# Expert rows weighed inside the expert loop, and the two rows of a token added on GpSimd ahead of the last normalization

## The reference

```
x: 6250 nodes x 256, 100000 edges with 96 features, sorted by dst
n  = layernorm(x)
x1 = x + n + relu([n, sum, max, mean of the node's edges, u] @ W1 + b1) @ W2 + b2
h  = layernorm(x1)
logits = h @ gate_w + gate_b               # 16 experts
(v1, v2), (e1, e2) = top_k(logits, 2);  w = softmax([v1, v2])
moe = w[0] * expert(e1, h) + w[1] * expert(e2, h)      # expert(e, h) = relu(h @ w1[e] + b1[e]) @ w2[e] + b2[e]
y = h + moe
out = x1 + layernorm(y) * gamma + beta
```

## Time and profile before

| | value |
|---|---|
| median of 3 executions | 1328.63 us |
| the profiled execution | 1334.45 us, span 1332.7 us |
| PE busy | 1185.9 us (89%) |
| DVE / ACT / POOL busy | 788.0 / 646.1 / 773.3 us |
| expert loop, about | 772 to 1221 us |
| final stage, about | 1223 to 1333 us |

### The profile page before, as it was taken

How to read it: one execution, slowest core, us unless ns; L and a number is a source line. 1 busy time by engine, 2 the same in 40 slices (tenths; PEclk the granted TensorE clock), 3 DMA queues, 4 the chain that set the end, 5 groups by cost and what they waited for, 6 DMA issues and landing times.

```text
span 1332.7 us, 28448 instructions
## 1 busy us (share of the span) xinstructions
PE 1185.9 (89%) x6684; PEld 1003.7 (75%) x6685; DVE 788.0 (59%) x3039; ACT 646.1 (48%) x1969; POOL 773.3 (58%) x1061
## 2 busy tenths in 40 slices
PE   2003999999999999999999989999999999999798
PEld 1003888888888888878888888899999999997343
DVE  4999999899799899903534014542222222222886
ACT  5963556655665665655664332223333333333554
POOL 4876666666666667666754235556666666663222
PEclk7555999999999999989999989999999999998555
DMA  9986677768758775592110348856666666664763
GB/s 313 287 269 232 201 275 284 283 237 318 256 215 294 276 239 189 218 334 80 47 45 28 115 155 296 269 174 205 212 212 204 211 212 211 210 212 123 244 203 93
DMA packets 131029, 282.67 MB, mean 212 GB/s; under 512 B 25609, under 2 KB 38283, under 8 KB 130821
## 3 DMA queue, kind: packets, MB, share of 16 engines
q1 hardware_dynamic: 93937, 218.40, 48.3%
q0 software_dynamic: 26048, 43.47, 10.4%
q10 hardware_dynamic: 10964, 19.96, 4.4%
HBM read 167.27 MB, written 114.25 MB: 211 GB/s over the span
## 4 chain that ended last, share of the span: by engine, by line
PE 63%; DMA 10%; issue 9%; POOL 8%; ACT 7%; POOLq 2%; DVE 1%; ACTq 1%; SPq 0%; DVEq 0%
PE ps L1158 14%; PE ps L1166 13%; PE ps L1048 8%; PE ps L1034 7%; PE ps L1036 7%; DMA mem<-piece_carry,mem 4%; PE ps L1199 3%; PE ps L1201 3%; POOL mem L571 2%; POOL mem L572 2%; PE ps L1144 2%; DMA mem<-x_normed,mem 2%; DMA mem<-in_dst_dram,mem 2%; POOL mem L554 2%; ACT mem L728 1%
## 5 line engine op out<-in xcount | busy, mean ns | idle before, releaser
L924 ACT ACTIVATE mem<-ps,mem 128x128 f32<-128x128 f32 x452 | 128.9, 368 | 306.8 <-PE ps L1158 304.8
L1158 PEld LDWEIGHTS ps<-mem 128*128 128x128 f32 x1808 | 221.4, 194 | 7.9 <-issue 3.0
L1158 PE MATMUL ps<-mem 128*128 128x128 f32 x1808 | 223.9, 278 | 1.5 <-issue 1.5
L1034 PE MATMUL ps<-mem 128*128 128x250 f32 x800 | 208.5, 383 | 13.5 <-ACT mem L826 11.9
L1166 PE MATMUL ps<-mem 128*128 x904 | 215.7, 382 | 2.8 <-issue 2.6
L1253 DVE TENSOR_TENSOR_SCAN mem<-ps,mem 128x80 f32<-128x80 f32 x960 | 207.9, 297 | 0.3
L1257 DVE TENSOR_TENSOR_SCAN mem<-ps,mem 128x80 f32<-128x80 f32 x960 | 207.8, 302 | 0.0
L1036 PE MATMUL ps<-mem 128*128 128x250 f32 x800 | 204.4, 378 | 0.0
L664 POOL DMA_INDIRECT expert_rows<-mem x113 | 113.5, 1004 | 126.9 <-DVE mem L1515 112.6
L1048 PE MATMUL ps<-mem 128*125 128x256 f32 x800 | 181.0, 379 | 0.7 <-ACT mem L826 0.7
L1166 PEld LDWEIGHTS ps<-mem 128*128 128x128 f32 x904 | 163.5, 191 | 22.7 <-issue 4.9
(11 more groups left out here) (252 smaller groups left out, 1696.1 us busy)
## 6 DMA issues: line engine op xcount, KB each, us to landing
mem<-in_L_ffn_w_dram SPq DMA_DIRECT2D x129, 512.0 KB, 9.4
run_sum<-mem SPq DMA_DIRECT2D x80, 480.0 KB
run_max<-mem SPq DMA_DIRECT2D x80, 480.0 KB
mem<-in_edge_attr_dram SPq DMA_DIRECT2D x72, 480.0 KB, 8.0
mem<-expert_rows SPq DMA_DIRECT2D x22, 512.0 KB, 5.4
x_rows<-mem ACTq DMA_DIRECT2D x25, 256.0 KB, 4.0
x_normed<-mem ACTq DMA_DIRECT2D x25, 256.0 KB
mem<-in_x_dram ACTq DMA_DIRECT2D x24, 256.0 KB, 4.1
```

The source lines that it names most:

```text
L924: ins = act.activation(hT[b][:, c, :], bank(2 + b, c * P, (c + 1) * P), ACT.Relu, bias=eb1c[:, bass.ds(e, 1), c])
L1034: pe.matmul(h, W1x[:, c, hc * P:(hc + 1) * P], XT[b][:, c, :], start=(c == 0), stop=False)
L1158: ins = pe.matmul(bank(2 + b, f * P, (f + 1) * P), w1now[q][:, c, f * P:(f + 1) * P], XgT[b][:, c, :], start=(c == 0), stop=(c == DC - 1))
```

## The change

The weight of a row is now a property of its slot. The one-hot products carry two values, the code of the row and its weight: `hot_rows` writes a second scaled one-hot beside the first, `early_slots` multiplies 172 columns instead of 86, `late_slots` 118 instead of 59, and `slot_tables` stores the weights as `wslot`. For that the exponential and `choice_weights` are done in two parts: for the early tiles in ACT's step 20 and before DVE's first `hot_rows`, for the late ones after ACT's tile 13 and DVE's tile 16. In the loop ACT multiplies the result of `expert2` in PSUM by `wslot` (`weigh_y`), and `take_y`, which now waits for ACT, adds the bias times `wslot`. In the final stage GpSimd adds the two rows of a token (`sum_rows`; those of batch n+2 stand ahead of the gamma product of batch n), and DVE adds the sum with one instruction per batch. DVE's `finish(n-1)` now comes after `moments(n+1)`; before, `finish(n)` did. ACT does `normed_again(n+2)` behind `last_norm(n)`, where it did `normed_again(n+1)` ahead of `deviation(n)`.

```diff
-    SLOTS_AT = 352
+    SLOTS_AT = 320
+            def sum_rows(n):
+                a = 2 * (BATCHES[n][1] - BATCHES[n][0])
+                pool.wait_ge(fy_got[n % DEEP], (n // DEEP + 1) * 32)
+                pool.tensor_tensor(FY[n % DEEP][0][0:NT, 0:a], FY[n % DEEP][0][0:NT, 0:a], FY[n % DEEP][1][0:NT, 0:a], ALU.add).then_inc(f_sum, 1)
...
+            sum_rows(0)
+            sum_rows(1)
             for n in range(len(BATCHES)):
+                if n + 2 < len(BATCHES):
+                    sum_rows(n + 2)
                 times_gamma(n)
...
+            def odds(part):
+                c = (slice(LC, TILES), slice(0, LC))[part]
+                act.wait_ge(gap_ready, part + 1)
+                act.activation(v0[:, 1, c], v0[:, 0, c], ACT.Exp).then_inc(e_gap, 1)
...
+            def weigh_y(i, b):
+                act.wait_ge(y_psum, i + 3)
+                act.activation(bank(6 + b, 0, D), bank(6 + b, 0, D), ACT.Identity, scale=wslot[:, bass.ds(i, 1)]).then_inc(y_weighed, 1)
+
+            def expert_step(i, g, b):
+                expert_relu(i, g, b)
+                weigh_y(i - 1, 1 - b)
...
             normed_again(0)
+            normed_again(1)
             for n in range(len(BATCHES)):
-                if n + 1 < len(BATCHES):
-                    normed_again(n + 1)
                 deviation(n)
                 last_norm(n)
+                if n + 2 < len(BATCHES):
+                    normed_again(n + 2)
...
-                        ins = pe.matmul(bank(7, SLOTS_AT, SLOTS_AT + KINDS), OL[n % HOT][:, m, :], OH[n % HOT][:, m, :],
+                        ins = pe.matmul(bank(7, SLOTS_AT, SLOTS_AT + 2 * KINDS), OL[n % HOT][:, m, :], OH[n % HOT][:, m, :],
...
-                pe.matmul(bank(5, P, P + OPEN), VT, Sel, start=True, stop=False)
+                pe.matmul(bank(5, P, P + 2 * OPEN), zeros[0:NT, 0:P], ones[0:NT, 0:2 * OPEN], start=True, stop=False)
+                for n in range(2):
+                    pe.matmul(bank(5, P + n * OPEN, P + (n + 1) * OPEN), VT[:, n], Sel, start=False, stop=False)
...
-                    st.mark(dve.scalar_tensor_tensor(out=high[n % HOT][:, m, :], in0=numbers[0:NT, 0:kinds], scalar=hi[:, kk, j:j + 1],
-                                                     in1=code[:, kk, c0 + j:c0 + j + 1].to_broadcast([NT, kinds]), op0=ALU.is_equal, op1=ALU.mult))
+                    for half, value in enumerate((code, wsel)):
+                        st.mark(dve.scalar_tensor_tensor(out=high[n % HOT][:, m, half * kinds:(half + 1) * kinds], in0=numbers[0:NT, 0:kinds], scalar=hi[:, kk, j:j + 1],
+                                                         in1=value[:, kk, c0 + j:c0 + j + 1].to_broadcast([NT, kinds]), op0=ALU.is_equal, op1=ALU.mult))
...
+                op(dve.tensor_copy(wslot[:, c], weight))
...
             places((Oa, Ob), rank, Rk, loq, hiq)
+            choice_weights(early, 0)
...
-                dve.wait_ge(y_psum, i + 3)
+                dve.wait_ge(y_weighed, i + 1)
                 if not isinstance(i, int) or i >= 2:
                     dve.wait_ge(yo_stored[b], g * 16)
-                dve.tensor_tensor(YO[b], bank(6 + b, 0, D), eb2bc[:, bass.ds(e, 1), :].rearrange("p o d -> p (o d)"), ALU.add).then_inc(y_ready, 1)
+                dve.scalar_tensor_tensor(out=YO[b], in0=eb2bc[:, bass.ds(e, 1), :].rearrange("p o d -> p (o d)"), scalar=wslot[:, bass.ds(i, 1)],
+                                         in1=bank(6 + b, 0, D), op0=ALU.mult, op1=ALU.add).then_inc(y_ready, 1)
...
                     late_experts(1)
+                    choice_weights(late, 1)
...
-            def add_expert(n, kk):
+            def add_experts(n):
...
+                dve.wait_ge(f_x2, n + 1)
+                dve.wait_ge(f_sum, n + 1)
+                f1.mark(dve.tensor_tensor(FS[b][:, 0:a], FS[b][:, 0:a], FY[n % DEEP][0][0:NT, 0:a], ALU.add))
                 f1.wait()
...
-            add_expert(0, 0)
-            add_expert(0, 1)
+            last = len(BATCHES) - 1
+            add_experts(0)
             moments(0)
             for n in range(len(BATCHES)):
-                if n + 1 < len(BATCHES):
-                    add_expert(n + 1, 0)
+                if n < last:
+                    add_experts(n + 1)
                 scale_shift(n)
-                if n + 1 < len(BATCHES):
-                    add_expert(n + 1, 1)
+                if n < last:
                     moments(n + 1)
-                finish(n)
+                if n:
+                    finish(n - 1)
+            finish(last)
```

More of the change, by code:

```diff
@@ L220, in gnn_moe_kernel @@
         wsel = k.take(2, TILES, parts=NT)
+        wslot = k.take(SLOT_TILES)
         IX = k.take(TILES, 2, parts=NT, dt=U32)
@@ L293, in gnn_moe_kernel @@
         OL = [a.take(OB, P, parts=NT) for _ in range(HOT)]
-        OH = [a.take(OB, KINDS, parts=NT) for _ in range(HOT)]
+        OH = [a.take(OB, 2 * KINDS, parts=NT) for _ in range(HOT)]
         a = Area(mem, WORK_END, TOTAL)
@@ L386, in gnn_moe_kernel @@
         fy_got = [sem(f"final_y_got{i}") for i in range(DEEP)]
-        f_x2, f_step, f_read, f_var, f_sd, f_stat, f_norm, f_scaled, f_z, f_out = (sem(f"final_{n}") for n in ("x2", "step", "y_read", "var", "sd", "stat", "norm", "scaled", "residual", "out"))
+        f_x2, f_sum, f_step, f_read, f_var, f_sd, f_stat, f_norm, f_scaled, f_z, f_out = (sem(f"final_{n}") for n in ("x2", "sum", "step", "y_read", "var", "sd", "stat", "norm", "scaled", "residual", "out"))
         pads_zeroed = sem("pads_zeroed")
@@ L917, in _ @@
                 gnn_step(i, i // 2, i % 2)
-            in_pairs(act, MACROS, lambda i, g, b: gnn_step(i, g, b, EARLY_M + MACROS - i), ahead=3, first=EARLY_M + 2)
+            for i in range(EARLY_M + 2, MACROS):
+                gnn_step(i, i // 2, i % 2)
+                if i == EARLY_M + 2:
+                    odds(0)
             def expert_relu(i, g, b):
@@ L934, in _ @@
             expert_relu(1, 0, 1)
+            weigh_y(0, 0)
             write_x2(MACROS - 1)
@@ L937, in _ @@
             expert_relu(2, 1, 0)
+            weigh_y(1, 1)
             take_x2(MACROS - 1, 4)
@@ L940, in _ @@
             take_logits(MACROS - 1, 5)
+            weigh_y(2, 0)
             for i in range(4, 14):
-                expert_relu(i, i // 2, i % 2)
-            act.wait_ge(gap_ready, 1)
-            act.activation(v0[:, 1, :], v0[:, 0, :], ACT.Exp).then_inc(e_gap, 1)
-            in_pairs(act, SURE, expert_relu, first=14)
+                expert_step(i, i // 2, i % 2)
+            odds(1)
+            in_pairs(act, SURE, expert_step, first=14)
             act.wait_ge(texp_ready, 2)
-            in_pairs(act, SLOT_TILES, expert_relu, first=SURE)
+            act.wait_ge(slots_ready, 2)
+            in_pairs(act, SLOT_TILES, expert_step, first=SURE)
+            weigh_y(SLOT_TILES - 1, 1 - SLOT_TILES % 2)
             def normed_again(n):
@@ L1388, in slot_tables, with gap, choice_weights @@
                 dve.sem_inc(slots_ready, 1)
+            def gap(c):
+                op(dve.tensor_tensor(v0[:, 0, c], v0[:, 1, c], v0[:, 0, c], ALU.subtract))
+                dve.sem_inc(gap_ready, 1)
+            def choice_weights(c, part):
+                dve.wait_ge(e_gap, part + 1)
+                op(dve.tensor_scalar(tB[:, c], v0[:, 1, c], 1.0, None, ALU.add))
+                op(dve.reciprocal(wsel[:, 0, c], tB[:, c]))
+                op(dve.tensor_tensor(wsel[:, 1, c], wsel[:, 0, c], v0[:, 1, c], ALU.mult))
             dve.wait_ge(chunk_done, CHUNKS)
@@ L1407, in _ @@
             column_sums(EC, Oa, Ob, both, cum, keepm)
+            gap(early)
             dve.wait_ge(prefix_out, 1)
@@ L1453, in late_columns @@
             def late_columns():
-                op(dve.tensor_tensor(v0[:, 0, :], v0[:, 1, :], v0[:, 0, :], ALU.subtract))
-                dve.sem_inc(gap_ready, 1)
+                gap(late)
                 column_sums(LC, OaL, ObL, bothL, cumL, keepL)
```

46 lines of the change are left out of this document (18 added, 28 removed).

## The result

The changed kernel takes **1347.9 us** (median of 4, 1343.73 to 1350.47) against 1328.63: ratio **1.0139, 95% interval [1.0104, 1.0175]**. Its profiled execution took 1347.38 us (span 1345.7, granted clock 0.911), 12.9 us over the one of before. The prediction was 1340.8 with 1332 to 1350.

What follows compares the result with a forecast made beforehand. TensorE was taken as the bound, full in the expert loop and at 4.0 us a macro in the final stage. Terms 4.6 + 0.4 + 2.3 + 0 + 4.9 = +12.2 us on the 1328.63 median gave 1340.8, range 1332 to 1350.

Steps and rivals of the forecast that it cites:

- Early one-hot products: Graph network: 144 TensorE instructions at 172 columns take 0.145 us instead of 0.113, +4.6 us, bounds 0 and 14.6.
- Late products and tile 18: Late products of 118 columns cost nothing more; four more instructions at tile 18 cost +0.4 us.
- late work in the loop: Expert loop tiles with late VectorE work behind take_y, tile 16 above all: +2.3 us, bounds 0.7 and 3.9.
- Steady tiles: Expert loop: ScalarE's step makes outputs 0.65 us later, covered by GpSimd's 1.19 us wait before the scatter: +0.
- What is relieved: Final stage: VectorE's 2.1 us less a round and GpSimd's relief are worth 0, since TensorE's 8.0 us covers them.
- First `finish`: Start of the final stage: the first finish ends later and TensorE's 22 macros start with it, +4.9 us, bounds 4.0 and 6.5.
- The clock: Rival: full clock returns in the final stage, other engines' rounds of 5.8 us bound it, 24 us less, 1317; chance 0.04.
- the real bound: Rival: VectorE, not TensorE, bounds the final stage, so 2.1 us a round is gained, about 1316; chance 0.05.
- wide products: Rival: 172 columns cost what 86 do and the loop's waits are absorbed, only 0.4 + 4.9 stay, 1334; chance 0.13.

Runs made afterwards that it cites:

- e3: Changed kernel with one-hot products as narrow as before (86 and 59 columns) and a constant 0.5 as every slot's weight; ratio 1.0089.
- after: The changed kernel itself, first measurement, against the kernel before; 1347.9 us, ratio 1.0139.
- e1: Changed kernel with the final stage's order on GpSimd, ScalarE and VectorE put back, so the first finish comes early; ratio 1.0155.
- e4: Changed kernel with TensorE's final-stage work halved, beta added by a last row of one matrix product; ratio 1.0011, slow executions left out.
- e5: The changed kernel itself measured again, unaltered; ratio 1.0167.
- e11: Changed kernel with beta as a last row of the residual's product and scale and shift ahead of the next sum; ratio 1.0204, including a misplaced wait.
- e9: Kernel before with only the change's final stage, the two rows added unweighted; ratio 1.0048.
- e6: Kernel before with one addition: ScalarE passes each tile's output through PSUM at scale 1.0 and VectorE waits for it; ratio 1.0024.
- e2: Changed kernel without ScalarE's step in the expert loop; VectorE makes bias times weight ahead, while expert2 runs; ratio 1.0105.
- e7: Changed kernel with GpSimd's scatter of a tile's outputs sent one step later; ratio 1.0157, slow executions left out.
- e8: Kernel before with TensorE's final-stage work halved, beta added by a last row of one matrix product; ratio 1.0086, slow executions left out.

## Why the prediction was right, and where it was off

**Early one-hot products, +4.6.** Right, 5.0 to 5.1: 0.150 us each, VectorE never late. e3 gives it back.

**Late products and tile 18, +0.4; late work in the loop, +2.3.** The wait at tile 16 is 1.49 us (some 1.7 foreseen), 1.1 more than before. By tile 26 the two profiled executions are 0.3 us apart, but the one of before had lost some 7 us at the loop's start (its first product of the loop was 7.2 us ahead), so these terms aren't settled by the pair.

**Steady tiles, "+0".** This is the step that failed. The 0.65 us that I gave ScalarE's step was right in size (0.66 to 0.76 measured). I set it against GpSimd's wait of 1.19 us before the scatter and called it covered. But that wait ended *with* the outputs, 0.99 us behind VectorE in both kernels: it was no slack, it moved with them, and each gather behind the scatter moved too. The lead fell by 1.2 us, 0.7 of it from this and 0.5 from the idle time ahead of the gathers, for which no run shows a cause. A gather that is held up by something else, mostly at the same tiles, then finds less reserve: 6.6 to 9.9 us lost in the runs of the changed kernel (after, e1, e3, e4, e5, e11), against 0.6. e5 shows that it repeats, e3 that it isn't the one-hot products, e9 that it isn't the final stage, e6 that half of it comes with ScalarE's step alone. That the lead is the reason is argued and not shown: e2 and e7 brought most of it back and lost 9.0 and 6.6 us. What holds up those gathers is open too.

**What is relieved, 0.** Right, and the least obvious term: B is 88.8 with VectorE busy for 73 or 52 us of 88. e4 and e8 show the other side, 22 us once TensorE isn't in front; I had written about 25.

**First `finish`, +4.9.** Right in mechanism, 6.6 in size (26.75 less 20.65 is 6.1 in e5, 5.8 in e9). GpSimd starts on batch 1 14.1 us after the last product (13.6 in e5), as VectorE did before (14.1). GpSimd's sum of 1024 elements takes 2.34 us and not 1.99, and `scale_shift` is held for 1.45 us by the sum of the next batch; from `normed_again` on, the chain took 4.4 us where I had 4.6.

**The sum.** +12.2 predicted, +12.9 for the profiled pair, 18.5 [13.8, 23.2] by the ratio. The pair agrees with the sum by a coincidence: loss +6 and `finish` +1.7 more than foreseen, and the one-hot products cancelled by before's bad start of the loop. With the terms as measured, 5.1 + 6.0 + 6.6, it is 17.7, which the ratio's interval holds. That 1347.9 lies inside 1332 to 1350 is in part luck: the forecast had the loop's loss at nothing. The bounds of its terms, added up, give 1333 to 1355, and its stated range was tighter than that.

**The rivals.** The clock stayed at 0.50 in the changed kernel. The Trainium skill (TensorE: Matmul & The Clock Gate, The HAM clock gate) has activity release the throttle; a TensorE busy for 87.85 of 88 us at 0.50 disagrees with it. VectorE wasn't the real bound (B unchanged), wide products weren't free. A fourth thing I had not weighed at all: VectorE and GpSimd getting in each other's way. It cost the first `finish` 1.45 us.

## What to carry to other kernels

A wait that ends with the very thing you delay is no slack: look at how far ahead of need the work *behind* that wait begins, and take that lead as a thing to measure, not as the whole cause (here two runs with most of it back lost as much). Taking work off an engine that is busy for 83% of a stage brings nothing while another is full; lighten both together or neither, and expect a next bound: here a ring through two engines at 70.0 us of 88.8, then at 65.9 partly the transfers. And compare stage by stage before believing that a profiled pair confirms a sum: here two errors of 6 and 5 us cancelled.
